# A graph kernel's first node stage rewritten: bias as a product with ones, halves from a temporary, normalised rows written during the first stream

## What is computed

```
x = layernorm(x + layer(x))
```

```
agg = segment_sum(x[src], dst)
h = relu((x + agg) @ W1.T + b1)
x = layernorm(x + relu(h @ W2.T + b2))
```

## Time and profile before

| | us |
|---|---|
| median of 3 runs | 2764.97 (2762.37 to 2767.31) |
| the profiled execution | 2763.7 |
| its span, first to last instruction | 2761.8 |
| mean granted TensorE clock | 0.981 of full speed |
| PE busy | 2588.5 (94%) |
| DVE busy | 1497.3 (54%) |
| ACT busy | 630.1 (23%) |
| POOL busy | 185.5 (7%) |

### The profile page before, as it was taken

How to read it: one execution, slowest core, us unless ns; L and a number is a source line. 1 busy time by engine, 2 the same in 40 slices (tenths; PEclk the granted TensorE clock), 3 DMA queues, 4 the chain that set the end, 5 groups by cost and what they waited for, 6 DMA issues and landing times.

```text
span 2761.8 us, 41946 instructions
## 1 busy us (share of the span) xinstructions
PE 2588.5 (94%) x16397; PEld 1474.6 (53%) x16397; DVE 1497.3 (54%) x5476; ACT 630.1 (23%) x732; POOL 185.5 (7%) x123
## 2 busy tenths in 40 slices
PE   0699999966999999999999999999999999999998
PEld 0367666643555555556555555555555555554455
DVE  5999999957677756667665533333222212222222
ACT  1488999951000011111111100000000000000000
POOL 3400000002000001111111100000000100000000
PEclk9699999988999999999999999999999999999999
DMA  7147444436999988888888789888888888888996
GB/s 216 47 183 167 175 169 181 183 146 219 340 339 346 311 289 297 301 298 280 308 287 300 262 276 311 275 276 265 276 275 274 268 276 275 275 262 293 289 293 218
DMA packets 234791, 712.59 MB, mean 258 GB/s; under 512 B 42427, under 2 KB 57487, under 8 KB 231129
## 3 DMA queue, kind: packets, MB, share of 16 engines
q1 hardware_dynamic: 200400, 638.43, 69.8%
q10 hardware_dynamic: 33384, 69.45, 7.3%
q0 software_dynamic: 800, 1.94, 0.2%
HBM read 617.83 MB, written 91.93 MB: 257 GB/s over the span
## 4 chain that ended last, share of the span: by engine, by line
PE 76%; DVE 18%; DMA 3%; ACT 1%; DVEq 1%; issue 1%; POOL 0%; SPq 0%; ACTq 0%; POOLq 0%
PE PS L1469 70%; DVE S L794 8%; DVE S L793 7%; DMA HR<-adjacency 2%; PE PS L1637 1%; DMA XN<-in_x_dram 1%; PE PS L1644 1%; PE PS L1645 1%; PE PS L1659 1%; DMA S<-adjacency 0%; PE PS L1642 0%; PE PS L1641 0%; POOL TB L563 0%; PE PS L1591 0%; PE PS L1668 0%
## 5 line engine op out<-in xcount | busy, mean ns | idle before, releaser
L1469 PE MATMUL PS<-HR,HN 128*128 128x500 f16 (+1 forms) x3864 | 811.5, 365 | 5.6 <-DMA HR<-adjacency 3.5
L1469 PE MATMUL PS<-HR,AGN 128*128 128x500 f16 (+1 forms) x3682 | 737.2, 344 | 8.8 <-DMA HR<-adjacency 8.6
L1469 PEld LDWEIGHTS PS<-HR,HN 128*128 128x128 f16 x3864 | 369.0, 96 | 397.1 <-issue 7.7
L1469 PEld LDWEIGHTS PS<-HR,AGN 128*128 128x128 f16 x3682 | 353.4, 97 | 304.7 <-issue 8.7
L794 DVE TENSOR_SCALAR S<-S,RBW 128x245 f16<-128x245 f16 x1250 | 424.4, 494 | 0.0
L793 DVE TENSOR_SCALAR S<-iot,RBW 128x128 f16<-128x128 f16 x1250 | 416.7, 467 | 2.0 <-PE PS L1469 1.7
L1469 PE MATMUL PS<-S 128*128 128x245 f16 x1250 | 337.7, 277 | 30.3 <-DVE S L794 27.5
L970 DVE TENSOR_SCALAR AT<-PS,SC 128x384 f32<-128x384 f32 (+24 forms) x100 | 43.3, 473 | 514.3 <-PE PS L1469 497.0
L1469 PE MATMUL PS<-S,HN 128*128 128x500 f16 (+1 forms) x1232 | 270.5, 370 | 2.1 <-DMA S<-adjacency 2.1
L1469 PEld LDWEIGHTS PS<-S 128*128 128x128 f16 x1250 | 120.1, 97 | 154.4 <-DVE S L794 35.2
L1469 PE MATMUL PS<-S,AGN 128*128 128x500 f16 (+1 forms) x924 | 201.7, 368 | 0.0
(11 more groups left out here) (227 smaller groups left out, 2068.9 us busy)
## 6 DMA issues: line engine op xcount, KB each, us to landing
HR<-adjacency SPq DMA_DIRECT2D x441, 875.0 KB, 5.3
S<-adjacency SPq DMA_DIRECT2D x147, 875.0 KB, 5.4
adjacency<-HN SPq DMA_DIRECT2D x9, 3062.5 KB, 9.6
AT<-source_lanes ACTq DMA_DIRECT2D x49, 544.0 KB, 6.7
AT<-in_edge_attr_dram ACTq DMA_DIRECT2D x48, 544.0 KB, 5.4
adjacency<-HR SPq DMA_DIRECT2D x8, 3062.5 KB, 10.0
adjacency<-TB SPq DMA_DIRECT2D x8, 3062.5 KB, 9.8
HR<-adjacency SPq DMA_DIRECT2D x42, 437.5 KB, 4.1
```

Source lines behind the costliest of these rows:

```text
L1469: return t_.matmul(out_, w, m, start=start, stop=True, skip_group_check=True)
```

## The change

Six edits, all about the node stage and what stands around it.

1. Bias b2 becomes a PE product: behind each of the 49 row products stands one of a row of ones with the bias row (one partition deep), added in PSUM. DVE's addition (L866) goes.
2. DVE's `factors_0` also makes `RD` = reciprocal * c1 and `BD` = -mean * RD. ACT's `high_0` writes scaled normalised rows with them to a temporary T0 in TB (seven operations) and copies T0 to `HI[1]` in one operation of 896 columns; `low_0` is one subtraction of 896 columns.
3. The normalised rows in XN are written by a new `normalise_0(q)` on ACT, at pieces 9, 11, ... 21 of the first stream. POOL's `bias_1` waits for the seventh.
4. The buffers `A16` swap HR and HN, so that the last slice lies in HR; SP's piece loads wait for its last product. DVE's wait before the stage is for the slices stored from HN.
5. The last slice's products are cut in three, with hidden 0, hidden 1 and rows 0 between; the flag is read and the branch taken ahead of them. `sub_sums(24)` on ACT stands behind high 1, and hidden 6 waits for it. ACT takes its branch before the stage rather than behind it.
6. `squares` on ACT waits for the last `low_0`; DVE drains before its prelude.

The diff, cut to these:

```diff
+        H0 = [TB[:, k * QN:(k + 1) * QN] for k in range(2)]
+        T0 = [TB[:, (2 + k) * QN:(3 + k) * QN] for k in range(2)]
+        RD, BD = (TB[:, 4 * QN + k * NB:4 * QN + (k + 1) * NB] for k in range(2))
-        A16 = [t[:, 0:NB * SD_ // 2].bitcast(f16) for t in (HN, HR, TB)]
+        A16 = [t[:, 0:NB * SD_ // 2].bitcast(f16) for t in (HR, HN, TB)]
-        X0 = [PS[:, 2560:2560 + UN], PS[:, 3072:3072 + UN]]
+        X0 = [PS[:, 2560:2560 + UN], PS[:, 3584:3584 + UN]]
...
                 sp.dma_start(RB, dinv_d.partition_broadcast(P)).then_inc(s_rb, 16)
+                sp.wait_ge(s_un, NS_)
...
             def bias_1():
-                pool.wait_ge(s_split, 2 * NQ)
+                pool.wait_ge(s_xn0, NQ)
...
                 dve.wait_ge(s_y0, q + 1)
-                v.tensor_tensor(three(y), three(y), bias(0, QB), ALU.add)
-                dve.drain()
                 v.scalar_tensor_tensor(out=XN[:, cols], in0=y, ...)
...
                 v.reciprocal(RS[:, bs], SD[:, bs])
                 dve.drain()
+                v.tensor_tensor(RD[:, bs], RS[:, bs], c1[:, bs], ALU.mult)
+                v.scalar_tensor_tensor(out=c2[:, bs], in0=MV[:, bs, 0], scalar=-1.0, in1=RS[:, bs], op0=ALU.mult, op1=ALU.mult)
+                dve.drain()
+                v.scalar_tensor_tensor(out=BD[:, bs], in0=MV[:, bs, 0], scalar=-1.0, in1=RD[:, bs],
                                        op0=ALU.mult, op1=ALU.mult).then_inc(s_nr0, 1)
...
             def low_0(q):
+                cols = slice(q * QN, (q + 1) * QN)
+                dve.wait_ge(s_hi, NQ + q + 1)
+                v.tensor_tensor(LO[1][:, cols], T0[q % 2], HI[1][:, cols], ALU.subtract).then_inc(s_split, 1)
...
-            dve.wait_ge(s_aw[0], 16 * len(range(0, NS_, 3)))
+            dve.wait_ge(s_aw[1], 16 * len(range(1, NS_, 3)))
...
             def high_0(q):
                 act.wait_ge(s_nr0, q + 1)
+                if q >= 2:
+                    act.wait_ge(s_split, NQ + q - 1)
+                for b in range(QB):
+                    k = q * QB + b
+                    c.activation(T0[q % 2][:, b * P:(b + 1) * P], XN[:, k * P:(k + 1) * P], ACT.Identity, bias=BD[:, k:k + 1], scale=RD[:, k:k + 1])
+                act.drain()
+                c.copy(HI[1][:, q * QN:(q + 1) * QN], T0[q % 2]).then_inc(s_hi, 1)
+
+            def normalise_0(q):
                 for b in range(q * QB, (q + 1) * QB):
                     x = XN[:, b * P:(b + 1) * P]
+                    last = c.activation(x, x, ACT.Identity, bias=c2[:, b:b + 1], scale=RS[:, b:b + 1])
+                last.then_inc(s_xn0, 1)
+
+            def stage_0(last_sums):
+                relu_0(0)
+                relu_0(1)
+                for q in range(NQ):
+                    root_0(q)
+                    if q + 2 < NQ:
+                        relu_0(q + 2)
+                    high_0(q)
+                    if q == 1 and last_sums:
+                        sub_sums(NS_ - 1)
...
             with act.Else():
+                stage_0(True)
+                act.wait_ge(s_lod, 32)
                 lanes(0)
...
+                    if n in range(9, 9 + 2 * NQ, 2):
+                        normalise_0((n - 9) // 2)
                     if n in LOOK_AT and LOOK_AT[n] + 2 < NG:
                         lanes(LOOK_AT[n] + 2)
...
+            def rows_0(q):
+                pe.wait_ge(s_tb0, q + 1)
+                if q >= 2:
+                    pe.wait_ge(s_yb0, q - 1)
+                for b in range(QB):
+                    y = Y0[q % 2][:, b * P:(b + 1) * P]
+                    t_.matmul(y, H0[q % 2][:, b * P:(b + 1) * P], WT[:, 1, :], start=True, stop=False)
+                    last = t_.matmul(y, ones[0:1, :], BR[0:1, 0, :], start=False, stop=True)
+                last.then_inc(s_y0, 1)
...
+            with pe.Else():
+                last_sub(0, NB // 3)
+                pe.wait_ge(s_at, NS_ - 1)
+                hidden_0(0)
+                last_sub(NB // 3, 2 * NB // 3)
+                hidden_0(1)
+                rows_0(0)
+                last_sub(2 * NB // 3, NB)
+                for q in range(1, NQ):
+                    if q + 1 < NQ:
+                        hidden_0(q + 1)
+                    rows_0(q)
```

More of the change, by code:

```diff
@@ L1272, in relu_0 @@
                 for h in range(2):
-                    last = c.activation(TB[:, (q % 2) * QN + h * UN:(q % 2) * QN + (h + 1) * UN], X0[h], ACT.Relu, bias=BC[:, 0:1])
+                    last = c.activation(H0[q % 2][:, h * UN:(h + 1) * UN], X0[h], ACT.Relu, bias=BC[:, 0:1])
                 last.then_inc(s_tb0, 1)
@@ L1282, in high_0 @@
                 act.wait_ge(s_nr0, q + 1)
+                if q >= 2:
[6 more added lines that the diff above has]
+            def normalise_0(q):
                 for b in range(q * QB, (q + 1) * QB):
                     x = XN[:, b * P:(b + 1) * P]
[L1285 to L1298, removed]
+                    last = c.activation(x, x, ACT.Identity, bias=c2[:, b:b + 1], scale=RS[:, b:b + 1])
[10 more added lines that the diff above has]
+                        sub_sums(NS_ - 1)
             def squares():
+                act.wait_ge(s_split, 2 * NQ)
                 c.activation(Q[:, 0:4 * P], WN[:, 1:5, :].rearrange("p k f -> p (k f)"), ACT.Square)
@@ L1386, in edge_high @@
                              scale=SCE[:, k, 0:1]).then_inc(s_ahi, 1)
-            act.wait_ge(s_lod, 32)
             with act.If(flags["act"]):
+                sub_sums(NS_ - 1)
+                act.wait_ge(s_sq2, 1)
+                c.activation(SQ[:, :], c1[:, :], ACT.Sqrt).then_inc(s_sr2, 1)
+                stage_0(False)
+                for q in range(NQ):
+                    normalise_0(q)
                 for p in range(1, LASTP + 1):
@@ L1552, in _, with last_sub @@
             pe.wait_ge(s_at, NS_ - 2)
-            for k in range(NB):
-                sub_pass(NS_ - 1, k, k == 0)
-            sub_end(NS_ - 1)
+            def last_sub(k0, k1):
+                for k in range(k0, k1):
+                    sub_pass(NS_ - 1, k, k == 0)
+                if k1 == NB:
+                    sub_end(NS_ - 1)
             read_flag(pe, "pe")
@@ L1577, in turned_rows, with hidden_0 @@
                 pe.wait_ge(s_axf, n + NQ)
+            def hidden_0(q):
+                if q:
+                    pe.wait_ge(s_tb0, q)
+                if q == NQ - 1:
+                    pe.wait_ge(s_at, NS_)
+                for h in range(2):
+                    last = t_.matmul(X0[h], WT[:, 0, :], AT[:, q * QN + h * UN:q * QN + (h + 1) * UN], start=True, stop=True)
+                last.then_inc(s_hid0, 1)
+            def rows_0(q):
[7 more added lines that the diff above has]
+                last.then_inc(s_y0, 1)
             with pe.If(flags["pe"]):
+                last_sub(0, NB)
                 pe.wait_ge(s_at, NS_)
@@ L1584, in _ @@
                 turned_rows(0, HL[0], 1)
[L1587 to L1602, removed]
-                    last = t_.matmul(Y0[q % 2][:, b * P:(b + 1) * P], TB[:, (q % 2) * QN + b * P:(q % 2) * QN + (b + 1) * P], WT[:, 1, :],
-                                     start=True, stop=True)
-                last.then_inc(s_y0, 1)
+                hidden_0(0)
+                for q in range(NQ):
+                    if q + 1 < NQ:
[4 more added lines that the diff above has]
+                pe.wait_ge(s_at, NS_ - 1)
+                hidden_0(0)
+                last_sub(NB // 3, 2 * NB // 3)
[3 more added lines that the diff above has]
+                for q in range(1, NQ):
+                    if q + 1 < NQ:
+                        hidden_0(q + 1)
+                    rows_0(q)
             def lengths():
```

15 lines of the change are left out of this document (2 added, 13 removed).

## The result

The changed kernel took 2794.84 us (median of 4 runs, 2793.45 to 2799.03) against 2765.98 for the kernel before beside it: 1.011 of its time, 95% interval 1.0095 to 1.0125, some 30 us slower. The forecast was 2761.2 (2755.5 to 2767.0), with 0.08 on slower. The profiled execution took 2799.03 us, its span is 2797.3, its mean granted clock 0.972.

A forecast was written before the change was run, and what follows sets the result against it. PE was taken to bound the kernel overall, but the node stage to be a chain between engines. Lookup 0 8.6 us earlier, less 4.8 in the first stream, gave -3.8 from 2764.97: 2761.2 us (2755.5 to 2767.0).

The forecast's parts named there:

- so depth saves nothing and I charge the 14 added instructions like the old ones: Node stage, PE's rows: one-partition products cost as much as full-depth ones, 1.65 us a group (0.8 to 2.9).
- each round begins with PE at 1.2 GHz after an idle time: Node stage rounds: idle PE starts slow, so hidden takes 3.35 us against 1.77 at the high clock.
- a rival with 0.12: Node stage: busier PE stays at 2.4 GHz, saving 3.2 to 4 us in two rounds; 2757.4 us, chance 0.12.
- The slower rival: Node stage: added products keep PE at 1.2 GHz, rows cost 2.9 us more each, 11.6 in all; 2772.8 us, chance 0.07.
- the jump behind the stage: Stage start: PE's branch jump ahead of the last slice's products costs 1.77 us (0 to 2.5), starting them at 557.8.
- DVE's jump: Ahead of DVE's prelude, between its last low and lookup 0: about 1.0 us of a 3.3 us path.
- the tail: From DVE's rows 6 to the end of low_0(6): 14.3 us instead of 17.7, ending the stage 3.4 earlier.
- POOL as what slowed the prelude: Before lookup 0: DVE's slow casts are waits for POOL, which now comes later; the 49-column cast falls under 0.3 us.
- the price of POOL's additions in the stream: First stream, lookup at 736.42: POOL's bias_1 slows one DVE comparison and mask, 3.4 us falling on PE.
- both costs of the stream together: First stream: delayed lane loads and POOL's additions together cost 4.8 us (1.5 to 8.5).
- The late lane loads: First stream: normalisations ahead of ACT's loads delay them 0 to 2.9 us; at 1.5, PE waits some 1.1 more.
- its -3.8: Whole kernel: lookup 0 8.6 us earlier less 4.8 paid in the first stream, -3.8 us in sum.

The follow-up runs named there:

- experiment 4: Changed kernel with the bias laid in first by two wide products one partition deep, row products added after: 2777.83 us, 1.0049 of the kernel before.
- experiment 3: Changed kernel with the bias product at full depth, identity times the bias on all partitions: 2766.77 us, 1.0013 of the kernel before.
- experiments 1: Changed kernel with DVE adding the bias of the rows again and no products with ones: 2770.23 us, 1.002 of the kernel before.
- 6: Changed kernel with DVE adding the bias, PE's last slice back ahead of flag and jump, ACT's sub_sums(24) ahead of its stage: 2761.91 us, 0.9996 of the kernel before.
- 8: Changed kernel with DVE adding the bias, last slice still interleaved, PE's flag and jump one slice earlier: 2764.10 us, 0.9996 of the kernel before.
- experiment 2: Kernel before with only the products with ones in place of DVE's addition: 2797.03 us, 1.0112 of the kernel before.
- experiment 7: Kernel of experiment 6 with POOL's seven additions of bias 1 moved behind edge tiles 4 to 10 of pass 2: 2758.77 us, 0.9981 of the kernel before.

## Why the prediction was wrong

- **The price of the added products.** The step that failed is "so depth saves nothing and I charge the 14 added instructions like the old ones, 1.65 at the high clock (bounds 0.8 and 2.9)". They added 4.0 us a group at the high clock (5.72 for 1.72) and some 8 where it was low (about 10 for the 1.97 of the earlier trace rows). The earlier trace rows is two products of one partition on their own; its reading was right, and experiment 4 bears it out (1.77 us for four wide instructions of either depth). It says what one costs, not what the change from one depth to another costs, and here the depth changes with every product. None of the rows read before shows products of unlike depth in turn, so the upper bound of 2.9 had nothing to rest on. At full depth (experiment 3) the price was near the forecast: rows of 3.1 us (573.17 to 576.29), 1.4 added.
- **The clock.** From "each round begins with PE at 1.2 GHz after an idle time" a rival with 0.12 took it that a busier PE would be a faster one. The slower rival, "the added products keep PE at the low clock", named half of the mechanism at a fraction of its price: it has nothing of the lost overlap, which makes a group 5.7 us even at the high clock, and it counted 2.9 us more for four sets on the chain. With both effects PE's rows and hiddens filled all seven groups, DVE and ACT waited for them, and their savings were worth nothing.
- **The jump of PE.** It was taken as "the jump behind the stage", 1.77 us, with bounds of 0 and 2.5; it took 8.97. Before, the general branch was jumped over behind the last slice's 104 products and didn't show (0.56 us of idle time at 567.52, and that by ACT). The row that I took, 1.77, is another jump, without the reading of the flag and beside queued work. Whether the flag or the branch takes the 8.97 was not tried: they moved together. By experiments 1 and 6, and again by 1 and 8, its place is worth 6.6 us, with the cold start behind it (5.66 for 3.60) in that.
- **DVE's jump** was counted as 1.0; it was 4.57, and 5 us came back when it was moved under a wait. With the seven short operations of the old `low_0` ahead of it the gap was 1.04 us before and 1.24 in experiment 2; with the one wide subtraction it was 4.43 to 4.68 in all ten kernels that have it there. Whether the number of operations is why it grew was not tried.
- **Right, as far as the traces show it:** the tail (13.9 for 14.3); POOL as what slowed the prelude (0.18 for 2.05, and 2.05 again in experiment 2, where POOL's additions stand as before); the price of POOL's additions in the stream (a wait of 3.85 at 769.58 for one of 0.65, forecast 3.4; experiment 7 took back 3 to 4 us). For both costs of the stream together the profiled executions give 4.2 us, forecast 4.8. The late lane loads, which I had at 1.1 of these, show in DVE's waits (4.90 us at 737.87 against 3.76 before) and in none of PE's.
- Experiment 6 is the change without ones, without PE's jump in that place and without interleaving. The prediction has no sum for it. By its own terms I estimate one of about -4: two rounds 0.5 shorter each (1.65 less on PE, 1.15 more on DVE), 1.15 more in the tail and 0.5 less at the start, on its -3.8. Measured were about -1 us, between -3.6 and +1.4 by the interval, so it lies just outside. Its lookup 0 starts at 637.39, where 637.8 was forecast, but that is luck in part: DVE's jump was 3.4 us longer than counted, and its last slice ended earlier in that execution.

## What to carry to other kernels

Don't alternate float32 products of 128 columns of unlike depth: one of 1 or 64 partitions between full ones took away the overlap of the weight loads, and PE was at 1.2 GHz though it was never idle. Such a term is cheaper laid in first, in few wide products (2777.8 for 2794.8 us), and cheaper still at full depth (2766.8) or left to DVE (2770.2), which these runs can hardly tell apart. A jump over a large branch costs what is not covered when the engine reaches it: put it ahead of a wait or behind a long queue, never between a wait and the work that others wait for. Then look, since 104 queued products covered PE's jump in five kernels and left 2.7 us of it in two.

## What was not expected of the hardware

- The two instructions of a float32 product of 128 columns took 0.415 us when one partition or 64 alternate with 128, and 0.22 when all use 128.
- The granted clock fell from 2.4 to 1.2 GHz in the middle of an unbroken run of products (595 us, PE busy since 566.93), and was at 0.56 of full speed on the mean from 595 to 656.7 with PE all busy, in experiment 2 at 0.55 over 65 us. With the same products at full depth and more idle time it stood at 0.82 to 1.0.
- A jump over a large branch left PE idle for 8.96 to 8.99 us in five kernels, the reading of the flag included, and DVE for 4.43 to 4.68 in ten.
